# Graph network kernel on one core: degrees applied behind the matmuls in the second dense stage, normalisation on ScalarE, stages set further apart

## What is computed

```
def _mgcn_conv(x, edge_index, edge_type, rel, W_in, W_out, W_loop, b, n):
    m = x[src] * rel[edge_type]
    m = concatenate([m[:half] @ W_in, m[half:] @ W_out])
    norm = 1.0 / maximum(deg, 1.0)                     # deg: edges that end at a node
    agg = segment_sum(m * norm[dst][:, None], dst)
    return tanh(agg + x @ W_loop + b)
h = emb + res * _mgcn_conv(emb, ..., rel1, W_in1, W_out1, W_loop1, b1)
h = h + res * _mgcn_conv(h, ..., rel2, W_in2, W_out2, W_loop2, b2)
x = x + h @ mu_w + mu_b                                # x2
x = x + ffn(layernorm(x))                              # two experts for all nodes
```

## Time and profile before

| | us |
|---|---|
| median of three runs | 2920.09 |
| the profiled execution, device time | 2916.88 |
| its span in the trace | 2915.1 |
| second dense phase in the trace, first load issued to first DVE instruction of the next phase | 2347.4 to 2602.4 |
| of this, first `linear` matmul to the start of the last `columns_low` | 2361.5 to 2600.1 |

### The profile page before, as it was taken

One profiled execution on the slowest core, in us unless ns is written; L12 is line 12 of the kernel. 1 busy time (PEld: TensorE's weight loads), 2 busy tenths in 40 slices (PEclk: granted clock), 3 DMA queues, 4 the chain that ended last, 5 costly groups with the idle time before them and its releaser, 6 DMA issues. The chain is left out here.

```text
span 2915.1 us, 55660 instructions
## 1 busy us (share of the span) xinstructions
PE 2677.8 (92%) x20716; PEld 2527.6 (87%) x20716; DVE 2377.0 (82%) x3308; ACT 1847.0 (63%) x3125; POOL 1928.0 (66%) x2028
## 2 busy tenths in 40 slices
PE   2799999999999996979999999999999957759998
PEld 1699999999999996979999999999999957759998
DVE  5688888888888887968888888888888869966666
ACT  5676666666666664867766666766666634435543
POOL 3677777777777775557777777777777747742322
PEclk9999999999999998989999999999999979979999
DMA  7433333333333333443333333333333323331222
GB/s 231 137 104 106 107 106 106 107 106 106 106 106 106 106 107 88 152 136 105 106 106 106 107 106 105 107 106 106 106 107 106 106 91 109 112 123 55 65 67 70
DMA packets 163417, 313.21 MB, mean 107 GB/s; under 512 B 34381, under 2 KB 96269, under 8 KB 163189
## 3 DMA queue, kind: packets, MB, share of 16 engines
q0 software_dynamic: 79872, 218.21, 25.9%
q1 hardware_dynamic: 82389, 91.10, 9.6%
q10 hardware_dynamic: 928, 0.85, 0.1%
HBM read 264.16 MB, written 45.88 MB: 106 GB/s over the span
## 5 line engine op out<-in xcount | busy, mean ns | idle before, releaser
L609 PE MATMUL edge_rg<-edge_rel_hi,edge_hot 128*128 128x256 f32 x6656 | 1505.2, 289 | 22.1 <-DVE edge_hot L499 4.8
L609 PE MATMUL edge_rg<-edge_rel_lo,edge_hot 128*128 128x256 f32 x4992 | 1270.2, 283 | 0.0
L609 PEld LDWEIGHTS edge_rg<-edge_rel_hi,edge_hot 128*128 128x128 f32 x6656 | 1185.5, 192 | 80.8 <-DVE edge_hot L499 63.7
L432 POOL DMA_INDIRECT edge_xg<-h,src x832 | 788.4, 948 | 266.7 <-issue 218.1
L432 POOL DMA_INDIRECT edge_xg<-emb,src x832 | 789.1, 948 | 262.8 <-issue 222.1
L609 PEld LDWEIGHTS edge_rg<-edge_rel_lo,edge_hot 128*128 128x128 f32 x4992 | 957.2, 192 | 0.1
L449 ACT CAST edge_m_hi<-edge_rg 128x1024 fp32r<-128x1024 f32 x416 | 422.8, 1016 | 488.1 <-DVE edge_rg L508 488.1
L514 DVE TENSOR_TENSOR edge_m_lo<-edge_rg,edge_m_hi 128x1024 fp32r<-128x1024 f32 x416 | 509.6, 1225 | 223.5 <-ACT edge_m_hi L449 223.5
L456 ACT ACTIVATE edge_hot<-edge_typ,minus_type 128x512 fp32r<-128x512 f32 x832 | 527.0, 685 | 178.9 <-PE edge_typ L599 174.8
L499 DVE TENSOR_SCALAR edge_hot<-edge_typ,type_of 128x512 fp32r<-128x512 f32 x832 | 582.6, 742 | 7.7 <-ACT edge_hot L456 7.7
L508 DVE TENSOR_TENSOR edge_rg<-edge_xg,edge_rg 128x1024 f32<-128x1024 f32 x416 | 510.8, 1228 | 67.1 <-DMA edge_xg<-emb,src 19.6
(11 more groups left out here) (160 smaller groups left out, 3797.7 us busy)
## 6 DMA issues: line engine op xcount, KB each, us to landing
edge_xg<-emb,src POOLq DMA_INDIRECT x832, 2.7
edge_xg<-h,src POOLq DMA_INDIRECT x832, 2.8
set_x_rows<-in_x SPq DMA_DIRECT2D x25, 256.0 KB, 3.7
emb<-set_e_rows SPq DMA_DIRECT2D x25, 256.0 KB, 3.4
emb_t<-set_e_t SPq DMA_DIRECT2D x25, 256.0 KB, 2.9
dense_prev<-emb_t SPq DMA_DIRECT2D x25, 256.0 KB, 2.8
h_t<-dense_work SPq DMA_DIRECT2D x25, 256.0 KB, 2.0
h<-dense_work SPq DMA_DIRECT2D x25, 256.0 KB, 2.1
```

The costliest lines, as they stand in the source:

```text
L432: pool.indirect_dma_start(xg[:, GROUP * q + t, :], None, nodes, bass.IndirectOffsetOnAxis(ap=at, axis=0)).then_inc(gathered[q], 16)
L609: ins = pe.matmul(rg[q % 2][:, t, :], hot[:, q % 2, c, t * P:(t + 1) * P], part[:, c, :], start=(c == 0 and part is rel_hi), stop=(c == FULL))
```

## The change

Only the second dense phase is changed. Lists of stages and the functions in them, cut to the core:

```diff
+        own = lin if first else [s.ps(f"own{k}", [P, DC, CHUNK]) for k in range(2)]
...
-            xb = s.sb("xb", [P, 2, 2, DIM])
+            xb = s.sb("xb", [P, DEEP, 2, DIM])
-            h_parts = [s.sb(f"h{k}", [P, DC, CHUNK], F32R) for k in range(2)]
+            h_parts = [s.sb(f"h{k}", [P, 2, DC, CHUNK], F32R) for k in range(2)]
...
-                over_chunks(sp, (0, load), (3, load_x), (4, store_x2), deep=DEEP)
+                over_chunks(sp, (0, load), (2, load_x), (5, store_x2), deep=DEEP)
...
+            def inverse_deviation(c, b, n, d, m):
+                pool.wait_ge(var_done, 2 * c + 2)
+                wait_past(pool, rows_done, c - 1)
+                pool.tensor_tensor(rstd[:, b], var[:, b], K["minus_half"][:, 0:2], ALU.pow).then_inc(rstd_done, 1)
+                pool.wait_ge(rstd_done, c + 1)
+                pool.tensor_tensor(minus_mean[:, b], minus_mean[:, b], rstd[:, b], ALU.mult).then_inc(centred, 1)
...
-            over_chunks(pool, (3, h_low), (4, inverse_deviation), (1, previous_low), (3, add_bias),
-                        (5, columns_low), deep=DEEP)
+            over_chunks(pool, (4, inverse_deviation), (0, previous_low), (2, h_low), (2, add_bias), (6, columns_low), deep=DEEP)
...
+            def combine(c, b, n, d, m):
+                dve.wait_ge(lin_done, c + 1)
+                wait_past(dve, h_lo, c - 1)
+                dve.tensor_tensor(h_t[:, b], lin[b][:], degrees(c).unsqueeze(1).to_broadcast([P, DC, CHUNK]),
+                                  ALU.mult).then_inc(normed, 1)
+                dve.wait_ge(normed, c + 1)
+                dve.tensor_tensor(h_t[:, b], h_t[:, b], own[b][:], ALU.add).then_inc(combined, 1)
...
+                dve.wait_ge(mv_done, 2 * c + 2)
+                dve.tensor_scalar(var[:, b], mv[:, b, :, 1], EPS, None, ALU.add).then_inc(var_done, 1)
+                dve.tensor_scalar(minus_mean[:, b], mv[:, b, :, 0], -1.0, None, ALU.mult).then_inc(var_done, 1)
-            def normalize(c, b, n, d, m):
-                dve.wait_ge(rstd_done, 2 * c + 2)
-                wait_past(dve, tr_done, c - 1)
-                wait_past(dve, rows_out[b], 16 * n)
-                for j in range(2):
-                    ins = dve.tensor_scalar(rows[:, b, j], x2[:, b, j], mv[:, b, j, 0:1], rstd[:, b, j:j + 1],
-                                            ALU.subtract, ALU.mult)
-                ins.then_inc(rows_done, 1)
...
-                over_chunks(dve, (3, residual), (4, moments), (1, scaled_low), (4, normalize), (0, scale),
-                            (1, weights_low), deep=DEEP)
+                over_chunks(dve, (2, residual), (4, moments), (0, scaled_low), (0, weights_low), (1, combine),
+                            deep=DEEP)
...
-                over_chunks(pe, (0, linear), (1, project), (2, to_columns), deep=DEEP)
+                over_chunks(pe, (0, linear), (4, to_columns), (2, project), deep=DEEP)
...
+            def normalize(c, b, n, d, m):
+                act.wait_ge(centred, c + 1)
+                wait_past(act, tr_done, c - 1)
+                wait_past(act, rows_out[b], 16 * n)
+                for j in range(2):
+                    ins = act.activation(rows[:, b, j], x2[:, d, j], ACT.Identity, bias=minus_mean[:, b, j:j + 1],
+                                         scale=rstd[:, b, j:j + 1])
+                ins.then_inc(rows_done, 1)
...
-                over_chunks(act, (3, tanh), (1, first_high), (1, previous_high), (3, h_high), (1, later_high),
-                            (5, copy_columns), deep=DEEP)
+                over_chunks(act, (2, tanh), (0, previous_high), (2, h_high), (0, scaled_high), (0, first_high),
+                            (4, normalize), (6, copy_columns), deep=DEEP)
```

More of the change, by code:

```diff
@@ L824, in _ @@
                 sp.wait_ge(rows_out[k], 16 * times)
-                sp.wait_ge(t_out[k] if first else x2_out[k], 16 * times)
+                if first:
+                    sp.wait_ge(t_out[k], 16 * times)
+            if not first:
+                for d in range(DEEP):
+                    sp.wait_ge(x2_out[d], 16 * -(-(CHUNKS - d) // DEEP))
         @block.gpsimd
@@ L943, in linear @@
                     pe.wait_ge(scaled_lo[h], c + 1)
-                wait_past(pe, tanh_done, 2 * c - 2)
+                if first:
+                    wait_past(pe, tanh_done, 2 * c - 2)
+                else:
+                    wait_past(pe, combined, c - 1)
                 for o in range(DC):
@@ L948, in linear @@
                     for k in range(DC):
-                        product(pe, lin[b][:, o, :], [v[:, 2, k, cols] for v in w],
-                                [v[:, b, k] for v in prev_parts], k == 0, False)
+                        product(pe, own[b][:, o, :], [v[:, 2, k, cols] for v in w],
+                                [v[:, b, k] for v in prev_parts], k == 0, not first and k == DC - 1)
                     for h in range(2):
@@ L953, in linear @@
                             ins = product(pe, lin[b][:, o, :], [v[:, h, k, cols] for v in w],
-                                          [v[:, b, h, k] for v in scaled], False, h == 1 and k == DC - 1)
+                                          [v[:, b, h, k] for v in scaled], not first and h == 0 and k == 0,
+                                          h == 1 and k == DC - 1)
                 ins.then_inc(lin_done, 1)
@@ L1006, in scaled_high @@
             def scaled_high(c, b, n, d, m):
+                if not first:
+                    wait_past(act, lin_done, c - 1)
                 for h in range(2):
-                    wait_apart(act, scaled_done, 2 * c + h + 1, act_passed)
+                    if first:
+                        wait_apart(act, scaled_done, 2 * c + h + 1, act_passed)
                     act.copy(scaled[0][:, b, h], sums(h, c).rearrange("p n k -> p k n")).then_inc(scaled_hi, 1)
@@ L1034, in tanh @@
                 else:
-                    wait_past(act, h_lo, c - 1)
+                    act.wait_ge(combined, c + 1)
                 for o in range(DC):
-                    act.activation(h_t[:, b, o], lin[b][:, o, :], ACT.Tanh, bias=b_sb[:, o:o + 1]).then_inc(tanh_done, 1)
+                    act.activation(h_t[:, b, o], lin[b][:, o, :] if first else h_t[:, b, o], ACT.Tanh,
+                                   bias=b_sb[:, o:o + 1]).then_inc(tanh_done, 1)
             def copy_rows(c, b, n, d, m):
```

49 lines of the change are left out of this document (26 added, 23 removed).

## The result

The changed kernel takes 2897.18 us (median of 4 runs, 2895.29 to 2898.93), the kernel before 2919.06 over its 4 runs. The ratio is 0.9925 with a 95% interval of 0.9908 to 0.9942: 21.9 us faster, clear of the 0.2% that a measurement here can tell. The forecast was 2900, with a range of 2872 to 2916.

A forecast was written before the change was run, and what follows sets the result against it. DVE was taken as the bound, replaced after the change by a ring through ACT at 8.15 us per turn. Start, turns and drain summed to 219.9 us against 239.8, a gain of 20: 2900 us, range 2872 to 2916.

The forecast's parts named there:

- a ring through ACT: Second dense phase: residual, moments, POOL's pair, normalize, copy_columns, tanh, next residual form the longest ring, 8.15 us per turn.
- The turn: Residual to next residual in the middle of the phase: 8.15 us, against 9.33 in the kernel before.
- The collision: Residual on DVE meets POOL's add_bias with 0.9 us to go, ends 0.55 us after it, 0.7 us late.
- Start: Start of the phase: ACT rounds chunk 0 before the weights, first matmul 0 to 1.8 us later, 0.6 taken.
- Drain: End of the phase, after chunk 24's residual: some 22 us against 14.8, from the longer lag.
- PE costs nothing: PE's regrouped matmuls and transposes cost nothing: 7.2 us per turn at the granted 0.92, with a cover of 2 us.
- The clean ring: Rival: POOL holds up neither its short pair nor residual; turn 6.7 us, 2872 us; chance 0.24.
- L897 above 1.2 us mean: Sign of the forecast: the residual on DVE (L897) would take over 1.2 us in the mean.
- The full clash: Rival: residual pays all of 1.04 us and L772 meets previous_low; about 9.0 us per turn, 2916 us; chance 0.14.
- Table switches: Rival: ACT loads tables between tanh and Identity, 1.28 us each, 2.56 us per turn, 2961 us; chance 0.05.
- 5.4 us off and 1.7 on: DVE per turn: normalize, its wait and scaling removed, 5.41 us; combine 1.4 and two small instructions 0.3 added.
- 19 full turns: Middle of the phase: 19 turns at the ring's pace of 8.15 us, 154.9 us in all.

The follow-up runs named there:

- the copies first: The change with copy_columns put ahead of normalize in ACT's list: 2875.01 us, ratio 0.9852 to the kernel before.
- copies and weights first: The change with copy_columns ahead of normalize, weights split first, copy_columns and columns_low at lag 5: 2882.47 us, 0.9880 of the kernel before.
- the extra copy: The change with one more ACT copy of 128x512 per turn, behind copy_columns and ahead of the next tanh: 2919.93 us, 1.0007 of the kernel before.
- normalize on ACT alone: The kernel before with only normalize moved to ACT, in front of copy_columns, old lags kept: 2910.35 us against 2921.80, ratio 0.9958.
- the degrees with the new lags alone: The change with normalize back on DVE, degrees behind the matmuls and new lags kept: 2926.59 us against 2921.80 for the kernel before, ratio 1.0016.
- moments first: The change with moments ahead of residual in DVE's list: 2908.99 us, ratio 0.9956 to the kernel before.
- the sums scaled first: The change with sums scaled ahead of the matmuls again, combine gone, normalize on ACT and new lags kept: 2913.28 us, 0.9973 of the kernel before.

## Why the prediction was right, point by point

- **The bound moves from DVE to a ring through ACT.** Shown. The brackets of the rows name each handover; a copy added in the ring costs 22 us and beside it none; cutting the ring gains 21 us.
- **The turn: 8.15 forecast, 7.83 measured.** The members, forecast and then measured in the turn shown: residual to the statistics' end, without POOL's delay, 2.8 and 2.72; the residual's delay by POOL 0.7 and 0.29 (0.37 one turn on); POOL's pair 1.85 and 1.62; normalize 0.75 and 0.99; copy_columns 1.2 and 1.19; tanh 0.9 and 0.94. Two terms were clearly too high and one too low. The tanh row was not a good neighbour for normalize: with pointers for scale and bias one instruction takes 593 ns in the mean. `combine` was 681 and 686 ns where L904's 675 was taken.
- **The collision.** That the residual would meet add_bias, and end 0.55 us after it, was right to the instruction (2483.44 against L865's end at 2482.89). Where it meets it was off: 0.9 us of add_bias were to be left, and 0.56 were. The Trainium skill, "SBUF — State Buffer", section "Who interferes with whom", has the later instruction wait until the earlier one ends. That would be from 2482.33 to 2482.89, then the free residual's 0.74, 1.30 us in all; the row says 1.11, so the wait is some 0.2 us shorter than by its words. By the same section a DVE instruction with one operand in PSUM is free of it, and the runs agree: the two instructions of `combine` took 0.68 to 0.69 us every time, in all ten other kernels that have them too.
- **Start +0.6, measured +1.8,** at the far end of what was allowed. ACT waited for the load of chunk 0 of h until 2361.22, and only then split the weights. This term was undersized, by 1.2 us.
- **Drain +7.2, measured +8.4.** The mechanism was right: the last copies and their low parts go one by one behind normalize.
- **PE costs nothing.** Right for its time. It waits 1.5 us per turn for previous_low, and `linear` is through 1.8 us before DVE's combine takes its result (2477.06 and 2478.86), where 2 us were forecast. Its clock was granted in full, which I had not counted on; with this cover it can have given little, which is argued and was not tried.

```profile
2480.45 0.39 PE L140 MATMUL dense_own<-dense_prev,dense_w 128*128 128x256 f32 x1 [1.54 <-POOL dense_prev L845]
```

- **The clean ring** did not come about, in the change or in its faster variants: with POOL busy 88% of the stretch (96% with the copies first) the residual nearly always meets something there, and takes 0.95 to 1.15 us in the change from chunk 3 on, up to 1.87 in the version with copies and weights first. The sign "L897 above 1.2 us mean" was missed for the same reason as the 8.15: the mean is 1.00. **The full clash** did come about for the residual, in the run with the extra copy (1.65 to 1.86 us), and there the whole gain was gone, 0.5 us per turn by the copy itself and 0.65 by the clash.
- **Table switches**: no ACT_TABLE_LOAD stands in the phase; tanh and Identity alternate without one, so this rival is out. This agrees with the Trainium skill, "ScalarE: Activation LUTs", section "Table sets: the hidden batching unit".
- **Degrees.** I had priced both parts by DVE's time alone, 5.4 us off and 1.7 on. What a part gains was never DVE's time: the runs show 11.5 us in all for normalize on ACT alone, a loss of 4.8 for the degrees with the new lags alone, 21.9 together.

That the sum comes within 3 us is in part luck, since errors of opposite sign cancel. The 19 full turns took 148.4 us where 154.9 was forecast, and the two turns without copies 12.7 where 14 was. Against this, the first two turns took 15.4 us where 12.2 was forecast: I had only left moments out of them, and without moments DVE waits for scaled_high and meets POOL, as in the run with moments first. Start and drain took 2.4 us more than forecast. The mechanism, the ring and its order, was right: in every full turn DVE waits 2.0 to 2.3 us for tanh, which stands behind the copies.

## What to carry to other kernels

When each engine works through a hand-written list, the pace of a turn is the longest ring of waits that runs through these lists, and it can be longer than any engine's work. Write the ring down, and put every entry that is not a link of it into the idle time ahead of a link: here two entries swapped on ACT were worth as much as the whole change. Before moving an entry, ask of it both questions, what it waits for and who stands behind it; and where two engines share a way into memory, expect that any shift of some tenths of a microsecond moves where they meet.

## What was not expected of the hardware

- The price of a collision between DVE and POOL is set by where in POOL's instruction DVE's begins, with 0.53 to 0.55 us in the rows read from the end of POOL's instruction to the end of the residual. The same instruction, the residual, took 0.75 us alone and 0.97, 1.11, 1.27, 1.54 and 1.83 us in turns of five kernels. 1.25 us of work less on POOL made a turn 0.28 us longer.
- The small DVE instruction on 128x2 (L935, adding epsilon) took 0.17 us in the change's middle turns and 0.69 in the version with the copies first, where POOL was in the middle of columns_low (its row stands there). So it is held up too, although it has only one tensor to read, and the two that `combine` added never were.
- The granted clock went from 0.92 to 1.00 in the middle of the phase. PE's busy share does not tell why: it was 79% before and 82% after, and over the same 50 us the sums scaled first had 82% at 0.90, normalize on ACT alone 79% at 1.00. PE's gaps had become shorter (1.5 us where 2.7 was seen), but that this is the cause is not shown.
